# A decoder block on one core: the row tiles' normalization in the pooling stage, on GpSimd in place of VectorE

## The reference, cut to what matters

```python
x = x + _L0_attn_ref(_layernorm(x, axis=-1), ...)              # stage A: x is (8, 256, 1024)
x = x + _L0_xattn_ref(_layernorm(x, axis=-1), ctx_4096, ...)   # stage B: pooling and gating
x = x + _L0_ffn_ref(_layernorm(x, axis=-1), gate_w, expert_w)  # stage C: 8 experts, 2 per token

def _L0_xattn_ref(x, channel_map, conv_w, bn_gamma, bn_beta):  # channels are the 256 positions
    mask = ...top k of channel_map over the channels, for each of the 1024 columns
    crucial_features = mask * x
    subcrucial_features = (1.0 - mask) * x
    c_max, c_avg = max and mean of crucial_features over the channels
    s_max, s_avg = max and mean of subcrucial_features over the channels
    A_S1 = _norm_active(_conv1d([c_max, c_avg], conv_w), bn_gamma, bn_beta)
    A_S2 = _norm_active(_conv1d([s_max, s_avg], conv_w), bn_gamma, bn_beta)
    return crucial_features * A_S1 + subcrucial_features * A_S2
```

## Time and profile before

| | |
|---|---|
| time, median of 3 runs | 1149.03 us (1147.2 to 1155.45) |
| the profiled execution: time, span | 1146.74 us, 1144.7 us |
| busy in the span: TensorE, VectorE, ScalarE, GpSimd | 1019.4, 570.0, 402.6, 480.3 us |
| the pooling | 420 to 512 us of the span |

### The profile page before, as it was taken

One profiled execution on the slowest core, in us unless ns is written; L12 is line 12 of the kernel. 1 busy time (PEld: TensorE's weight loads), 2 busy tenths in 40 slices (PEclk: granted clock), 3 DMA queues, 4 the chain that ended last, 5 costly groups with the idle time before them and its releaser, 6 DMA issues. The chain is left out here.

```text
span 1144.7 us, 13559 instructions
## 1 busy us (share of the span) xinstructions
PE 1019.4 (89%) x3534; PEld 534.3 (47%) x3535; DVE 570.0 (50%) x1661; ACT 402.6 (35%) x1142; POOL 480.3 (42%) x662
## 2 busy tenths in 40 slices
PE   6788789899998779899755999999999999999995
PEld 6686445455554445434433444444444444444442
DVE  5645679898787778987987111111121211111111
ACT  2435788797777317857730000000000000000000
POOL 3833566566665100105614443333334444443331
PEclk9878899998899889989976999999999999999998
DMA  8410111110000322001597346373737346373332
GB/s 304 137 58 0 48 47 38 32 62 1 1 1 1 147 75 74 1 1 79 231 361 281 80 131 177 75 220 73 220 73 215 79 117 187 82 229 80 74 73 37
DMA packets 38463, 120.25 MB, mean 105 GB/s; under 512 B 6220, under 2 KB 9351, under 8 KB 38408
## 3 DMA queue, kind: packets, MB, share of 16 engines
q1 hardware_dynamic: 25592, 79.77, 18.9%
q0 software_dynamic: 12816, 39.86, 15.9%
HBM read 82.91 MB, written 36.70 MB: 104 GB/s over the span
## 5 line engine op out<-in xcount | busy, mean ns | idle before, releaser
L2012 PE MATMUL bank<-T,X 128*128 x1184 | 508.7, 592 | 0.0
L2012 PEld LDWEIGHTS bank<-T,X 128*128 128x128 f32 x1184 | 225.1, 190 | 283.5 <-issue 283.5
L2074 DVE TENSOR_SCALAR X<-bank,col_p 128x512 f32<-128x512 f32 x37 | 27.8, 751 | 400.7 <-PE bank L2012 400.7
L2040 ACT ACTIVATE X<-bank,col_p 128x512 f32<-128x512 f32 x37 | 25.4, 687 | 495.5 <-PE bank L2012 495.5
L1965 POOL DMA_INDIRECT X<-x_nrm,col_s x156 | 150.0, 962 | 71.5 <-issue 46.9
L1974 POOL DMA_INDIRECT out_dram<-X,col_d x37 | 60.0, 1622 | 263.6 <-DVE X L2074 251.1
L816 ACT ACTIVATE M<-X,T 128x256 bf16<-128x256 f32 x200 | 98.6, 496 | 0.5
L451 POOL TENSOR_TENSOR T<-T 128x8 f32<-128x8 f32 x216 | 88.0, 408 | 16.3
L640 PE MATMUL bank<-nat,T 128*128 128x512 f32 x128 | 73.6, 710 | 6.7 <-ACT X L804 3.8
L460 POOL TENSOR_TENSOR rs<-ve,neg_half 128x4 f32<-128x4 f32 x36 | 37.3, 1035 | 79.5 <-DVE ve L955 79.1
L217 POOL TENSOR_TENSOR late<-late,neg_half 128x1 f32<-128x1 f32 x32 | 17.5, 548 | 116.1 <-DVE late L213 116.1
(11 more groups left out here) (333 smaller groups left out, 1459.4 us busy)
## 6 DMA issues: line engine op xcount, KB each, us to landing
T<-in_L_ffn_expert_w_dram SPq DMA_DIRECT2D x8, 4096.0 KB, 17.5
out_dram<-X SPq DMA_DIRECT2D x17, 512.0 KB
M<-in_x_dram SPq DMA_DIRECT2D x16, 512.0 KB, 7.2
X<-in_x_dram SPq DMA_DIRECT2D x16, 512.0 KB, 5.2
x_nrm<-H SPq DMA_DIRECT2D x16, 512.0 KB, 3.5
T<-in_ctx_dram SPq DMA_DIRECT2D x9, 512.0 KB, 3.7
X<-x_nrm,col_s POOLq DMA_INDIRECT x156, 3.6
X<-in_ctx_dram SPq DMA_DIRECT2D x4, 512.0 KB, 7.0
```

The costliest lines, as they stand in the source:

```text
L2012: mm = nc.tensor.matmul(bank[2 * u + n][:, :], xgt[u][:, k, :], Tf[:, ds(odd * D + (k * N + n * BANK), BANK)], start=(k == 0), stop=(k == ...
```

## The change

The normalization of a row tile leaves VectorE's loop and is issued by GpSimd, right behind the root of the same tile. It is one instruction as before, with the same operands and the same two operations; its waits (the ring, the root) go with it. The roots of tiles 0 and 1 are taken in the block before, so GpSimd's loop begins with two normalizations.

```diff
             @block.gpsimd
             def _(pool):
-                for t in range(CT, NT):
-                    ln_pow(pool, 0, t)
+                def normed(t):
+                    if t >= 2:
+                        hold(pool, x1_tp, (t - 1) * KU)
+                    hold(pool, ln_rstd, t + 1)
+                    nc.gpsimd.tensor_scalar(ring[t % 2], X[:, t, :], mean_of(0, t), rstd_of(0, t), ALU.subtract, ALU.mult).then_inc(ln_out, 1)
+
+                for t in range(NT):
+                    if t >= CT:
+                        ln_pow(pool, 0, t)
+                    normed(t)
...
-                def normed(t):
-                    if t >= 2:
-                        hold(dve, x1_tp, (t - 1) * KU)
-                    dve.wait_ge(ln_rstd, t + 1)
-                    v.tensor_scalar(ring[t % 2], X[:, t, :], mean_of(0, t), rstd_of(0, t), ALU.subtract, ALU.mult).then_inc(ln_out, 1)
-
                 for t in range(NT + LAG + 1):
                     if CT <= t < NT:
                         hold(dve, x1_done, 2 * t + 2)
                         ln_stats(dve, 0, t)
                     if 0 <= t - LAG < UNITS:
                         crucial(t - LAG)
-                    if t < NT:
-                        normed(t)
                     if 0 <= t - LAG - 1 < UNITS:
                         maxima(t - LAG - 1)
```

## The result

The changed kernel takes 1157.77 us (median of 19 runs, 1152.75 to 1166.97) where the kernel before takes 1149.46 us (19 runs): a ratio of 1.0077, 95% interval 1.0058 to 1.0097, or 8.9 us. One of the 19 runs before took 1366.33 us; such a slow run is not in the ratio. It is slower, by more than four times the 2.0 us that I forecast.

The account below looks back on a forecast made before the run. VectorE was taken to bound the pooling: normalizations off its path save 8.0 us, stops by GpSimd cost 9.7, the start 0.3, in all +2.0 us, from 1149.03 to 1151.0 us. The range was 1141 to 1164 us.

Parts of the forecast that it names:

- What bounds the kernel: Pooling: VectorE is the path from step 5 on, at 5.56 us a step against TensorE's 4.74.
- as late as VectorE but no later: Pooling without the normalizations: VectorE's step falls to 4.83 us, about TensorE's 4.74, so TensorE does not hold it up.
- the second chain: End of the pooling: TensorE's last router products, 10.47 us up to 511.61, run beside VectorE's path with almost no slack.
- I take D = 1.08 us: GpSimd's duration for one 128x1024 normalization, from the slope of two one-input selects, 0.83 ns an element.
- the upper end of 2.36: Longest duration allowed for GpSimd's normalization, 2.36 us, taken from the gating's 128x1024 product of two tensors.
- Each normalization costs VectorE D - 0.15 = 0.93 us: Pooling steps: VectorE's two-input instruction waits for GpSimd's whole normalization less 0.15 us start-up, 0.93 us in place of 0.73.
- At the start +0.3 us: Start of the pooling: TensorE gets its first tiles later from GpSimd and passes 0.3 us on to step 5.
- a drop of the clock: TensorE's clock in the pooling: no separate case, since the wait before the last tiles stays about as long.
- As a latency it is free: Pooling steps: the tile is normalized about 2.0 us behind its epsilon, now 2.35, so TensorE gets it no later.
- rival (a): Pooling: GpSimd is slow, D between 1.5 and 2.36 us, costing +6.8 to +18.0 us; chance 0.27.
- Rivals (b) to (d): Pooling: (b) VectorE not stopped, 1141.3; (c) GpSimd gets no turn, 1143; together 0.16; (d) no effect, 1149, 0.07.

Follow-up runs that it names:

- the order alone: Kernel before with all tiles normalized on VectorE and only the next tile's statistics moved between the pieces of `crucial`: ratio 0.9994.
- best kernel: Against the kernel before: tiles 5 to 13 normalized on GpSimd, the others on VectorE, statistics between the pieces of `crucial`; 1143.53 us, ratio 0.9945.
- the halves: Changed kernel with each normalization issued as two GpSimd instructions of 512 columns: 1159.43 us in one execution.
- the statistics between: Changed kernel, all 16 tiles on GpSimd, with VectorE's next-tile statistics between the second and third piece of `crucial`: ratio 1.0027 against the kernel before.
- the run that has this term alone: Only tiles 0 and 1 normalized on GpSimd, tiles 2 to 15 on VectorE: ratio 1.0048 against the kernel before.

## Why the prediction was right in sign and far off in size

**What bounds the kernel: right up to tile 13.** VectorE's step set the pace from step 5 on: 0.25 us off it by the order alone shortened each of ten steps by 0.25. (VectorE's 9.2 of 10 us holds from 450 us on; in the two windows before it is 8.35 and 8.54.) With the normalizations off, TensorE is not "as late as VectorE but no later": its tiles come at 4.79 us, not 4.74, and it takes over the pace. The best kernel's 6.3 us are near 9 x 0.73 = 6.6 by luck: in the ten steps the tiles give 4.8 us and the order 2.5, and 0.7 is lost again behind them. The end of the stage hangs on TensorE's way from tile 13 to tile 15, the second chain that the prediction saw and gave no term.

**"I take D = 1.08 us": the step that failed.** It measured 3.78 us undisturbed, and the upper end of 2.36 did not hold either. The slope that I took is that of two selects, which share the one input tensor with it and nothing else: they run at 0.83 ns an element, the tensor_scalar at 3.3; the tensor_scalar of 8 elements was too short to show it. The product of two tensors was no bound from above, because a tensor_scalar with a single constant already takes longer (2.77 against 2.34). The Trainium skill, "GPSIMD Engine Reference", section "3.1 Elementwise — side-by-side cycle accounting", gives 1.03 cycles an element for short bodies; the 3.3 ns an element measured here do not agree with it for this instruction.

**"Each normalization costs VectorE D - 0.15 = 0.93 us": the size by luck, the mechanism wrong.** 0.83 us was measured, but with D = 3.78 the rule as I put it says 3.63. VectorE is not stopped for the whole of GpSimd's instruction, only for some 0.8 ns per element; the halves show how long, and the statistics between show that it is near the start of GpSimd's instruction. It is about as long as a copy of the tile takes (1.04 us whole). That it is the time in which GpSimd reads its input fits all of this, but no run shows it directly. In the earlier trace rows VectorE was held nearly to the end of GpSimd's instruction, so that row could not tell the two apart. The rule of the Trainium skill ("SBUF — State Buffer", section "Who interferes with whom") holds for which instructions meet (two SBUF inputs stopped, the statistics with one not); that the second waits for the whole of the first does not hold here.

**"At the start +0.3 us": mis-sized, 5.8 us in the run that has this term alone.** The working had the form (2 D - 2.5); with D = 3.78 it gives 5.1, which is what TensorE's products are late (9.4 against 4.3 us); the clock, at half behind the pause of 9.61 us, makes the rest. That a drop of the clock was no case of its own was wrong too.

**"As a latency it is free": wrong through D.** The tile is ready 5.2 us behind its epsilon (496.41 to 501.60) instead of 2.35. In the middle of the loop nobody misses it. At the end TensorE's row of work starts with tile 13, and all behind it comes later, through ScalarE up to VectorE's 2.21 us in step 17. The prediction had the tile at TensorE no later than before, and so no term for this.

**Why the time still fell into the range.** Two errors worked against each other: rival (a), with its formula, would have given +36 us at D = 3.78 (13 D - 12.7). The range held for a reason that was not the prediction's. Rivals (b) to (d) are out: VectorE is stopped, GpSimd does get its turn, and the move does something.

## What to carry to other kernels

Price an instruction on GpSimd by a row with the same operation; another of the same shape and the same number of inputs can be 3.6 times off. Before a step goes to a slower engine, look at the iterations in which nothing hides it, the first ones and those on which the end of a second engine's work hangs: here the first 2 of 16 made nearly two thirds of the loss. Leaving five at the start and two at the end where they were, with VectorE's one-input work put behind the start of GpSimd's, turned 0.8% of loss into 0.55% of gain.

## What the runs showed of the hardware that I had not expected

- GpSimd, 128x1024 float32: copy 1.04 us, product of two tensors 2.34, tensor_scalar with one operation 2.77 to 2.84, with two 3.63 to 3.80. Constants or per-row scalars make 0.07 to 0.15 us of difference.
- A GpSimd tensor_scalar stops a VectorE instruction with two SBUF inputs for about 0.8 ns an element (0.83 us for 1024, 0.40 for 512). With 1024 elements it then works on for some 2.7 us (498.87 to 501.60) without stopping anything.
- In a full step GpSimd starts beside one of VectorE's instructions, two more of 0.35 us start and pass, and the next is stopped; GpSimd's instruction lasts 4.33 instead of 3.78 us. Why two more, no run here shows.
- Behind the pause in front of tile 13 the same eight router products took 3.60 us at a granted clock of 1.00, 4.16 at 0.85, 4.55 at 0.78, 5.39 at 0.66 and 5.53 at 0.65. That is up to 1.9 us at the end of the stage; what decides it, no run here shows.
